# The last stage of a four-layer kernel: who adds the tokens, how its small steps are grouped, how its rows lie in memory, who issues its stores

## The chip, the cores and the metric

The kernel runs on one core of a Trainium2 chip. A core has TensorE (matmuls, PE in the profile), VectorE (DVE), ScalarE (ACT), GpSimd (POOL) and SyncE (SP), which here only issues transfers, and 16 DMA engines. The engines run their own instruction streams and meet at semaphores. The metric is the time of one execution on the device in microseconds, the median of several runs; lower is better.

## The reference

The input is 16 batches of 512 tokens, each of 128 float32 values. Four sublayers follow one another, each closed by a residual and a layer norm: a selective state-space layer, a layer with the signs of a 128x128 weight, gated linear attention with 16 heads, and a mixture of eight experts, of which each token takes two. The change touches only what comes after the experts have computed:

```python
out = jnp.sum(combined.reshape(-1, TOPK, D), axis=1)   # the token's two weighted results
...
x = _layernorm(x + _L1_ffn_ref(x, ...), axis=-1)
# _layernorm: (x - mean) / sqrt(var + 1e-5), over the 128 values of a token
```

So for every token: first result + second result + the token itself, then mean and variance over 128 values, then scale and shift.

## The kernel before

A long loop over batches computes the first three sublayers and sends each token, with its shares, to two rows of a scratch tensor that is sorted by expert. The expert stage then takes 136 tiles of 128 such rows, computes the expert of each tile, scales the rows by their shares, and writes them to `results_scratch` with indirect stores from GpSimd (L1997): first the results of every token's one expert, behind them those of the other. Beside it SP loads all tokens of the third sublayer back into `tokens` (L679).

The last stage, the tail, starts when all of these stores have landed. It goes over the 16 batches. A batch is 128 partitions x 4 tokens x 128 values. Token number c*128 + p of a batch lies on partition p (`"b (c p) d -> b p c d"`, L407, L538, L539), so each partition reads and writes four separate rows of 512 bytes. For batch b, with slot n = b modulo 4:

- SP loads the two result blocks into `both[:, n]` (`load_both`, L692), four batches at the start; the load of batch b + 4 is issued after VectorE has read batch b (`s_mixed`). Between these loads SP issues the store of batch b (L696), after its normalization (`s_final`).
- GpSimd adds the tokens to the second result in place (`add_token`, L2012), two batches ahead.
- VectorE adds the two results into `final_in[:, n]` (`mix_results`, L1819) and takes the statistics of each of the four tokens with `bn_stats` (L1829). Seven small steps on 128x4 (L1832 to L1841, `final_deviation`) make from them minus the mean and the variance of all four.
- GpSimd raises the variance to the power -1/2 (L2022) and multiplies it by minus the mean (L2024) (`final_shift`).
- ScalarE computes `final = final_in * scale + shift`, one activation a token column, four a batch (`normalize_final`, L1346), after the store that last used the slot has landed.

`final_in`, `final` and the small tensors have four slots (`FINAL_SLOTS`), and so has `both`. VectorE's result add of batch b waits for the normalization of batch b - 4. The order of the work is written out by hand: each engine runs its own loop over batches, in the order in which the instructions stand, and `LN_STEPS = 11` counts the semaphore's steps per batch (4 statistics, 7 small steps).

Of the kernel before, what the change touches and what calls it, by code (L numbers as in the profile page):

```python
# [7 lines left out]
P = 128  # L8
T = 512
TILES = T // P  # L10
# [24 lines left out]
LN_STEPS = 11  # L35
RMS_EPS = float(np.finfo(np.float32).eps)
# [171 lines left out]
FINAL_SLOTS = 4  # L208

# [18 lines left out]
def build(nc, a, out):  # L228
# [6 lines left out]
    with ExitStack() as ctx:  # L235
# [32 lines left out]
        minus_half = sb_kept("minus_half", [P, TILES])  # L268
# [11 lines left out]
        def sem(name):  # L280
# [114 lines left out]
        both = sb_kept("both", [P, FINAL_SLOTS, 2, TILES, P])  # L395
# [11 lines left out]
        x3_dram = nc.dram_tensor("x3_scratch", [B, T, P], F32, kind="Internal").ap().rearrange(  # L407
            "b (c p) d -> b p c d", p=P)
# [104 lines left out]
        s_both = [sem(f"both_results_loaded{n}") for n in range(FINAL_SLOTS)]  # L513
# [24 lines left out]
        out_dram = out.rearrange("b (c p) d -> b p c d", p=P)  # L538
        both_dram = results_dram[0:2 * B * T, :].rearrange("(r b c p) d -> r b p c d", r=2, b=B, p=P)  # L539
# [36 lines left out]
        def _(sp):  # L576
# [102 lines left out]
            def load_tokens(b):  # L679
                sp.dma_start(tokens[:, bass.ds(b * TILES, TILES), :],  # L680
                             x3_dram[bass.ds(b, 1)].rearrange("b p c d -> (b p) c d")).then_inc(s_tokens, 16)
# [10 lines left out]
            def load_both(b):  # L692
                for r in range(2):
                    sp.dma_start(both[:, b % FINAL_SLOTS, r, :, :], both_dram[r, b]).then_inc(s_both[b % FINAL_SLOTS], 16)

            def store(b, n):  # L696
                sp.wait_ge(s_final, TILES * (b + 1))
                sp.dma_start(out_dram[bass.ds(b, 1)].rearrange("b p c d -> (b p) c d"), final[:, n]
                             ).then_inc(s_out[n], 16)
# [3 lines left out]
            for b in range(FINAL_SLOTS):  # L703
                load_both(b)
            for b in range(B):
                store(b, b % FINAL_SLOTS)
                if b + FINAL_SLOTS < B:
                    sp.wait_ge(s_mixed, b + 1)
                    load_both(b + FINAL_SLOTS)
# [340 lines left out]
        def _(act):  # L1050
# [295 lines left out]
            def normalize_final(b):  # L1346
                n = b % FINAL_SLOTS
                act.wait_ge(s_shifted, b + 1)
                after(act, s_out[n], 16 * (b // FINAL_SLOTS))
                for t in range(TILES):  # L1350
                    nc.scalar.activation(final[:, n, t, :], final_in[:, n, t, :], ACT.Identity, bias=shift4[:, n, t:t + 1],
                                         scale=rstd4[:, n, t:t + 1]).then_inc(s_final, 1)

            for b in range(B):
                normalize_final(b)


        @block.vector
        def _(dve):
# [459 lines left out]
            def mix_results(b):  # L1819
                slot = b % FINAL_SLOTS  # L1820
                after(dve, s_final, TILES * (b - FINAL_SLOTS + 1))
                dve.wait_ge(s_added, b + 1)
                nc.vector.tensor_tensor(final_in[:, slot], both[:, slot, 0], both[:, slot, 1], ALU.add).then_inc(s_mixed, 1)

            def final_deviation(b):
                n = b % FINAL_SLOTS
                dve.wait_ge(s_mixed, b + 1)
                for t in range(TILES):
                    nc.vector.bn_stats(stats4[:, n, t, :], final_in[:, n, t, :]).then_inc(s_ln4, 1)  # L1829
                after(dve, s_shifted, b - FINAL_SLOTS + 1)  # L1830
                dve.wait_ge(s_ln4, at(b, LN_STEPS, 4))
# [3 lines left out]
                dve.wait_ge(s_ln4, at(b, LN_STEPS, 6))  # L1835
                nc.vector.tensor_tensor(apart4[:, n], apart4[:, n], apart4[:, n], ALU.mult).then_inc(s_ln4, 1)
                nc.vector.tensor_scalar(mean4[:, n], mean4[:, n], -0.5, None, ALU.mult).then_inc(s_ln4, 1)
                dve.wait_ge(s_ln4, at(b, LN_STEPS, 8))
                nc.vector.scalar_tensor_tensor(var4[:, n], apart4[:, n], P / 4, var4[:, n], ALU.mult, ALU.add).then_inc(s_ln4, 1)
                dve.wait_ge(s_ln4, at(b, LN_STEPS, 10))  # L1840
                nc.vector.tensor_scalar(var4[:, n], var4[:, n], 1 / P, LN_EPS, ALU.mult, ALU.add).then_inc(s_ln4, 1)  # L1841

            for b in range(B):
                mix_results(b)
                final_deviation(b)
# [3 lines left out]
        def _(pool):  # L1849
            nc.gpsimd.memset(minus_half[:], -0.5).then_inc(s_prep, 1)  # L1850
# [16 lines left out]
            def scale_of(step, scale, it):  # L1867

                pool.wait_ge(step, at(it, LN_STEPS, LN_STEPS))
                nc.gpsimd.tensor_tensor(rstd[:], var[:], minus_half[:], ALU.pow).then_inc(scale, 1)  # L1870
# [141 lines left out]
            def add_token(b):  # L2012
                slot = b % FINAL_SLOTS
                pool.wait_ge(s_both[slot], 32 * (b // FINAL_SLOTS + 1))
                nc.gpsimd.tensor_tensor(both[:, slot, 1, :, :], both[:, slot, 1, :, :], tokens[:, b * TILES:(b + 1) * TILES, :],
                                        ALU.add).then_inc(s_added, 1)

            def final_shift(b):
                n = b % FINAL_SLOTS
                pool.wait_ge(s_ln4, at(b, LN_STEPS, LN_STEPS))  # L2020
                after(pool, s_final, TILES * (b - FINAL_SLOTS + 1))
                nc.gpsimd.tensor_tensor(rstd4[:, n], var4[:, n], minus_half[:], ALU.pow).then_inc(s_rstd4, 1)  # L2022
                pool.wait_ge(s_rstd4, b + 1)
# [7 lines left out]
            pool.wait_ge(s_tokens, 16 * B)  # L2031
            for b in range(2):
                add_token(b)
            for b in range(B):
                final_shift(b)
                if b + 2 < B:
                    add_token(b + 2)
# [63 lines left out]
```

## Time and profile before

| | us |
|---|---|
| median of 3 runs | 2409.65 (2407.55 to 2413.64) |
| the profiled execution | 2408.81 |
| its span, first to last instruction | 2406.9 |
| busy: PE, DVE, ACT, POOL | 2090.9, 1953.4, 1414.8, 804.8 |
| the tail's first load issued, from the span's start | 2341.09 |

The page cuts the span in 40 slices of 60 us; a digit is the busy share in tenths. TensorE stands at 8 to 9 in the expert stage and at 0 in the last slice, where VectorE has 8, GpSimd 7 and ScalarE 4. The tail is thus the last slice and a little more. A time without a unit is in microseconds from the span's start. In the rows, `x4` counts instructions that are merged into one row, `[... <-X]` is the idle time of the engine before the row and what ended it, and L numbers are lines of the kernel before.

### The profile page before, as it was taken

Reading aid. Unit: us, or ns where it says so; the run is one execution under the profiler, and the core shown is the slowest. Engines: PE = TensorE matmul, PEld = TensorE weight load, DVE = VectorE, ACT = ScalarE, POOL = GpSimd, SP = SyncE. Lnnn points to the kernel's source line nnn. Section 1 sums busy time; section 2 is a strip of 40 time slices with the busy share of each in tenths; the row PEclk is TensorE's granted clock in tenths of the full one; section 3 lists DMA queues with packets and bytes.
Section 4 is the critical chain, followed back from the end, with each engine's and each line's share of the span. In section 5 each row is a group of like instructions: output and inputs, shape, how many; then the busy total and the mean of one; then the engine's idle time right before and its main releaser. Section 6 shows DMA issues by size and latency. Waiting matters only on the chain.

```text
span 2406.9 us, 52418 instructions
## 1 busy us (share of the span) xinstructions
PE 2090.9 (87%) x15864; PEld 1548.4 (64%) x15865; DVE 1953.4 (81%) x3681; ACT 1414.8 (59%) x3240; POOL 804.8 (33%) x1060
## 2 busy tenths in 40 slices
PE   4589899898989898989898999989889669999980
PEld 2256666575656575757565666657576569999980
DVE  6788988888898889898889898888985467777768
ACT  3466666666766666666676666667656323333334
POOL 0011414142424243232414141414243233333337
PEclk7699999999999999999999999999999879999995
DMA  6342424334242434242415242433321132212226
GB/s 178 88 115 63 111 75 101 90 81 104 68 105 66 116 74 114 68 109 71 116 55 127 56 115 73 103 88 84 102 67 30 61 119 61 59 54 62 60 58 188
DMA packets 154382, 212.88 MB, mean 88 GB/s; under 512 B 20296, under 2 KB 88912, under 8 KB 153920
## 3 DMA queue, kind: packets, MB, share of 16 engines
q1 hardware_dynamic: 132048, 144.20, 20.3%
q0 software_dynamic: 22272, 67.92, 13.8%
q8 instruction: 31, 0.51, 0.1%
q14 instruction: 31, 0.25, 0.0%
HBM read 134.71 MB, written 28.08 MB: 68 GB/s over the span
## 4 chain that ended last, share of the span: by engine, by line
PE 58%; DVE 18%; issue 9%; ACT 9%; DMA 4%; POOL 2%; DVEq 1%; SPq 0%; ACTq 0%; POOLq 0%
PE banks L1011 8%; PE banks L747 5%; PE banks L856 4%; PE banks L851 4%; PE banks L1022 4%; PE banks L835 4%; PE banks L886 4%; PE banks L908 4%; PE banks L881 3%; PE banks L804 3%; DVE ch L1449 2%; DVE push L1434 2%; ACT S L1190 2%; DMA y<-ch 2%; DVE hs L1441 2%
## 5 line engine op out<-in xcount | busy, mean ns | idle before, releaser
L1441 DVE TENSOR_TENSOR_SCAN hs<-decay,push 128x512 f32<-128x512 f32 x256 | 312.5, 1243 | 5.4
L1190 ACT ACTIVATE S<-banks,fall_tok 128x128 f32<-128x128 f32 x1024 | 277.7, 384 | 28.2 <-PE banks L823 26.4
L1011 PE MATMUL banks<-rowsT,w_here 128*128 128x128 f32 x2176 | 269.5, 278 | 6.6 <-DVE w_here L1785 6.1
L1011 PEld LDWEIGHTS banks<-rowsT,w_here 128*128 128x128 f32 x2176 | 256.0, 193 | 10.2 <-issue 9.4
L1956 POOL TENSOR_TENSOR qd<-q,q_fall 128x512 f32<-128x512 f32 x96 | 161.6, 1683 | 237.2 <-ACT chunk_fall L1175 237.1
L1865 POOL DMA_DIRECT2D y<-ch x96 | 88.1, 918 | 450.6 <-DVE ch L1449 349.4
L1547 DVE TENSOR_TENSOR S<-banks,S 128x512 f32<-128x512 f32 x256 | 168.0, 683 | 71.3 <-PE banks L835 43.1
L1997 POOL DMA_INDIRECT results_scratch<-rows_out,result_to x136 | 131.9, 970 | 241.3 <-ACT rows_out L1316 234.3
L1305 ACT ACTIVATE tanh_h<-banks 128x512 f32<-128x512 f32 x136 | 81.3, 598 | 203.5 <-PE banks L1011 162.4
L1434 DVE TENSOR_TENSOR push<-du,b_all 128x1024 f32<-128x1024 f32 x128 | 186.5, 1457 | 5.0 <-DMA b_all<-bc_scratch 4.4
L835 PE MATMUL banks<-q,k 64*128 64x128 f32 x1024 | 147.6, 284 | 43.9 <-DVE state L1598 28.9
L1101 ACT ACTIVATE decay<-delta,a_neg 128x512 f32<-128x512 f32 x256 | 171.9, 729 | 19.8 <-DVE hs L1441 19.4
L1934 POOL DMA_INDIRECT rows_scratch<-x,row_now x128 | 167.9, 1312 | 40.0 <-issue 34.2
L804 PE MATMUL banks<-x2T,w_k 128*128 128x512 f32 x256 | 134.6, 607 | 45.6 <-DVE k L1540 45.6
L1449 DVE TENSOR_TENSOR ch<-hs,c_all 128x1024 f32<-128x1024 f32 x128 | 163.4, 1276 | 3.0 <-DMA y<-ch 0.9
L1554 DVE SCALAR_TENSOR_TENSOR oT<-tog,banks 128x512 f32<-128x512 f32 x128 | 87.4, 683 | 93.6 <-ACT sq L1158 93.6
L835 PEld LDWEIGHTS banks<-q,k 64*128 64x128 f32 x1024 | 123.5, 187 | 58.8 <-issue 48.2
L851 PE MATMUL banks<-w_v,x2T 128*128 128x512 f32 x256 | 148.9, 665 | 0.0
L836 PE MATMUL banks<-q,k 64*128 64x128 f32 x1024 | 148.2, 285 | 0.0
L1870 POOL TENSOR_TENSOR rstd<-var,minus_half 128x4 f32<-128x4 f32 x48 | 48.7, 1014 | 296.6 <-DVE var L1415 296.6
L908 PEld LDWEIGHTS banks<-w_o,oT 128*128 128x128 f32 x1024 | 124.0, 193 | 36.4 <-issue 34.3
L1158 ACT ACTIVATE sq<-banks 128x512 f32<-128x512 f32 x128 | 76.9, 601 | 116.4 <-PE banks L886 116.4
(218 smaller groups left out, 5177.5 us busy)
## 6 DMA issues: line engine op xcount, KB each, us to landing
y<-ch POOLq DMA_DIRECT2D x96, 512.0 KB
b_all<-bc_scratch SPq DMA_DIRECT2D x128, 256.0 KB, 4.9
c_all<-bc_scratch SPq DMA_DIRECT2D x128, 256.0 KB
q_fall<-fall_scratch SPq DMA_DIRECT2D x192, 128.0 KB, 3.2
rows_in<-rows_scratch SPq DMA_DIRECT2D x136, 66.0 KB
both<-results_scratch SPq DMA_DIRECT2D x32, 256.0 KB, 3.4
w<-w_dram SPq DMA_DIRECT2D x3, 2048.0 KB, 9.1
xT<-xT_dram SPq DMA_DIRECT2D x16, 256.0 KB, 3.1
```

What stands on the lines that cost most here:

```text
L804: pe.matmul(bank, w[:, u * P:(u + 1) * P], x2T[:], start=True, stop=True).then_inc(full, 1)
L835: even = pe.matmul(low[:, at_h], k[0:DH, pair, here], q[0:DH, pair, here], start=True, stop=True)
L851: pe.matmul(bank, x2T[:, here], w_v[:, f * T:(f + 1) * T], start=True, stop=True).then_inc(full, 1)
L908: pe.matmul(bank[:, 0:P], oT[:, t, :], w_o[:, t, :], start=(t == 0), stop=(t == PAIRS - 1))
L1011: mm = pe.matmul(bank_h[:, u % 2, n, here], w_here[:, u % 2, n, here], x, start=True, stop=True)
L1101: nc.scalar.activation(decay[:, n % 2, h, :], delta[:, h, :], ACT.Exp, scale=a_neg[:, h, n:n + 1]).then_inc(s_decay, 1)
L1190: ins = nc.scalar.activation(S[:, g, here], bank[:, here], ACT.Exp, bias=fall_tok[:, head:head + 1])
L1434: nc.vector.tensor_tensor(push[:], du[:], b_all[:, slot, :].unsqueeze(1).broadcast_to([P, HALVES, T]), ALU.mult).then_inc(s_push, 1)
L1441: nc.vector.tensor_tensor_scan(hs[:, h, :], decay[:, n % 2, h, :], push[:, h, :], 0.0, ALU.mult, ALU.add).then_inc(s_scan, 1)
L1449: nc.vector.tensor_tensor(ch[:, n % 2, :, :], hs[:], c_all[:, slot, :].unsqueeze(1).broadcast_to([P, HALVES, T]), ALU.mult).then_inc(s_ch, 1)
L1547: nc.vector.tensor_tensor(S[:, g, :], full(ring, f"S{g}_{c}", j), S[:, g, :], ALU.mult).then_inc(ring.free_sem(f"S{g}_{c}"), 1)
L1934: nc.gpsimd.indirect_dma_start(out=rows_dram, out_offset=bass.IndirectOffsetOnAxis(ap=row_now[:, n, t:t + 1], axis=0), in_=x3_rows[:, t, : ...
```

## The change

- `BOTH_SLOTS = 8`: `both` has eight slots; the others keep four. SP issues the loads of batch b after VectorE has read batch b - 8, and no stores.
- Four tokens in a row per partition: token 4p + c of a batch lies on partition p in the tail (`"b (p c) d -> b p c d"`), so each partition reads and writes one piece of 2048 bytes, in the loads of results and tokens and in the store. The scratch tensor of tokens is still written in the old order of partitions, and read in the new one.
- VectorE adds the tokens (`add_token` is now VectorE's). It works in pairs of batches: two result adds, two token adds, eight statistics, and then the seven small steps once, on 128x8 (`PAIR_STEPS = 15`).
- GpSimd has only the pow and the product left, once per pair, on 128x8.
- ScalarE issues the store of batch b - 1 after the activations of batch b.

```diff
 LN_STEPS = 11
+PAIR_STEPS = 15
 RMS_EPS = float(np.finfo(np.float32).eps)
...
 FINAL_SLOTS = 4
+BOTH_SLOTS = 8
 
...
         eye = sb_kept("eye", [P, P])
-        minus_half = sb_kept("minus_half", [P, TILES])
+        minus_halves = sb_kept("minus_halves", [P, 2, TILES])
+        minus_half = minus_halves[:, 0]
         rms_eps = sb_kept("rms_eps", [P, 1])
...
         rows_out = sb_kept("rows_out", [P, 2, MOE_LOAD, P])
-        both = sb_kept("both", [P, FINAL_SLOTS, 2, TILES, P])
+        both = sb_kept("both", [P, BOTH_SLOTS, 2, TILES, P])
         stats4 = sb_kept("stats4", [P, FINAL_SLOTS, TILES, 6])
...
         fall_dram = nc.dram_tensor("fall_scratch", [B, 2, TILES, PAIRS, P], F32, kind="Internal").ap()
-        x3_dram = nc.dram_tensor("x3_scratch", [B, T, P], F32, kind="Internal").ap().rearrange(
-            "b (c p) d -> b p c d", p=P)
+        x3_scratch = nc.dram_tensor("x3_scratch", [B, T, P], F32, kind="Internal").ap()
+        x3_dram = x3_scratch.rearrange("b (c p) d -> b p c d", p=P)
+        tokens_dram = x3_scratch.rearrange("b (p c) d -> b p c d", p=P)
         rows_dram = nc.dram_tensor("rows_scratch", [ALL_ROWS, ROW], F32, kind="Internal").ap()
...
         s_results = [sem("results_stored0"), sem("results_stored1")]
-        s_both = [sem(f"both_results_loaded{n}") for n in range(FINAL_SLOTS)]
+        s_both = [sem(f"both_results_loaded{n}") for n in range(BOTH_SLOTS)]
         s_mixed = sem("results_mixed")
...
         x_dram = a["x"].rearrange("b (c p) d -> b p c d", p=P)
-        out_dram = out.rearrange("b (c p) d -> b p c d", p=P)
-        both_dram = results_dram[0:2 * B * T, :].rearrange("(r b c p) d -> r b p c d", r=2, b=B, p=P)
+        out_dram = out.rearrange("b (p c) d -> b p c d", p=P)
+        both_dram = results_dram[0:2 * B * T, :].rearrange("(r b p c) d -> r b p c d", r=2, b=B, p=P)
         spare_dram = rows_dram[EXPERTS * REGION:ALL_ROWS, :]
...
                 sp.dma_start(tokens[:, bass.ds(b * TILES, TILES), :],
-                             x3_dram[bass.ds(b, 1)].rearrange("b p c d -> (b p) c d")).then_inc(s_tokens, 16)
+                             tokens_dram[bass.ds(b, 1)].rearrange("b p c d -> (b p) c d")).then_inc(s_tokens, 16)
 
...
             def load_both(b):
+                slot = b % BOTH_SLOTS
                 for r in range(2):
-                    sp.dma_start(both[:, b % FINAL_SLOTS, r, :, :], both_dram[r, b]).then_inc(s_both[b % FINAL_SLOTS], 16)
-
-            def store(b, n):
-                sp.wait_ge(s_final, TILES * (b + 1))
-                sp.dma_start(out_dram[bass.ds(b, 1)].rearrange("b p c d -> (b p) c d"), final[:, n]
-                             ).then_inc(s_out[n], 16)
+                    sp.dma_start(both[:, slot, r, :, :], both_dram[r, b]).then_inc(s_both[slot], 16)
 
             for n in range(2):
                 sp.wait_ge(s_results[n], 16 * MOE_LOAD * (ROW_TILES // MOE_BODY))
-            for b in range(FINAL_SLOTS):
+            for b in range(B):
+                after(sp, s_mixed, b - BOTH_SLOTS + 1)
                 load_both(b)
-            for b in range(B):
-                store(b, b % FINAL_SLOTS)
-                if b + FINAL_SLOTS < B:
-                    sp.wait_ge(s_mixed, b + 1)
-                    load_both(b + FINAL_SLOTS)
             for n in range(FINAL_SLOTS):
...
                 n = b % FINAL_SLOTS
-                act.wait_ge(s_shifted, b + 1)
+                act.wait_ge(s_shifted, b // 2 + 1)
                 after(act, s_out[n], 16 * (b // FINAL_SLOTS))
                 for t in range(TILES):
                     nc.scalar.activation(final[:, n, t, :], final_in[:, n, t, :], ACT.Identity, bias=shift4[:, n, t:t + 1],
                                          scale=rstd4[:, n, t:t + 1]).then_inc(s_final, 1)
 
+            def store(b):
+                n = b % FINAL_SLOTS
+                act.wait_ge(s_final, TILES * (b + 1))
+                act.dma_start(out_dram[b], final[:, n]).then_inc(s_out[n], 16)
+
             for b in range(B):
                 normalize_final(b)
+                if b:
+                    store(b - 1)
+            store(B - 1)
 
...
                 after(dve, s_final, TILES * (b - FINAL_SLOTS + 1))
+                dve.wait_ge(s_both[b % BOTH_SLOTS], 32 * (b // BOTH_SLOTS + 1))
+                nc.vector.tensor_tensor(final_in[:, slot], both[:, b % BOTH_SLOTS, 0], both[:, b % BOTH_SLOTS, 1], ALU.add
+                                        ).then_inc(s_mixed, 1)
+
+            def add_token(b):
+                slot = b % FINAL_SLOTS
+                dve.wait_ge(s_mixed, b + 1)
+                nc.vector.tensor_tensor(final_in[:, slot], final_in[:, slot], tokens[:, b * TILES:(b + 1) * TILES, :], ALU.add
+                                        ).then_inc(s_added, 1)
+
+            def final_stats(b):
+                slot = b % FINAL_SLOTS
                 dve.wait_ge(s_added, b + 1)
-                nc.vector.tensor_tensor(final_in[:, slot], both[:, slot, 0], both[:, slot, 1], ALU.add).then_inc(s_mixed, 1)
-
-            def final_deviation(b):
-                n = b % FINAL_SLOTS
-                dve.wait_ge(s_mixed, b + 1)
                 for t in range(TILES):
-                    nc.vector.bn_stats(stats4[:, n, t, :], final_in[:, n, t, :]).then_inc(s_ln4, 1)
-                after(dve, s_shifted, b - FINAL_SLOTS + 1)
-                dve.wait_ge(s_ln4, at(b, LN_STEPS, 4))
+                    nc.vector.bn_stats(stats4[:, slot, t, :], final_in[:, slot, t, :]).then_inc(s_ln4, 1)
+
+            def final_deviation(m):
+
+                n = slice(2 * m % FINAL_SLOTS, 2 * m % FINAL_SLOTS + 2)
+                after(dve, s_shifted, m - 1)
+                dve.wait_ge(s_ln4, at(m, PAIR_STEPS, 8))
                 nc.vector.tensor_tensor(mean4[:, n], stats4[:, n, :, 1], stats4[:, n, :, 4], ALU.add).then_inc(s_ln4, 1)
                 nc.vector.tensor_tensor(apart4[:, n], stats4[:, n, :, 1], stats4[:, n, :, 4], ALU.subtract).then_inc(s_ln4, 1)
                 nc.vector.tensor_tensor(var4[:, n], stats4[:, n, :, 2], stats4[:, n, :, 5], ALU.add).then_inc(s_ln4, 1)
-                dve.wait_ge(s_ln4, at(b, LN_STEPS, 6))
+                dve.wait_ge(s_ln4, at(m, PAIR_STEPS, 10))
                 nc.vector.tensor_tensor(apart4[:, n], apart4[:, n], apart4[:, n], ALU.mult).then_inc(s_ln4, 1)
                 nc.vector.tensor_scalar(mean4[:, n], mean4[:, n], -0.5, None, ALU.mult).then_inc(s_ln4, 1)
-                dve.wait_ge(s_ln4, at(b, LN_STEPS, 8))
+                dve.wait_ge(s_ln4, at(m, PAIR_STEPS, 12))
                 nc.vector.scalar_tensor_tensor(var4[:, n], apart4[:, n], P / 4, var4[:, n], ALU.mult, ALU.add).then_inc(s_ln4, 1)
-                dve.wait_ge(s_ln4, at(b, LN_STEPS, 10))
+                dve.wait_ge(s_ln4, at(m, PAIR_STEPS, 14))
                 nc.vector.tensor_scalar(var4[:, n], var4[:, n], 1 / P, LN_EPS, ALU.mult, ALU.add).then_inc(s_ln4, 1)
 
-            for b in range(B):
-                mix_results(b)
-                final_deviation(b)
+            dve.wait_ge(s_tokens, 16 * B)
+            for m in range(B // 2):
+                for step in (mix_results, add_token, final_stats):
+                    for b in (2 * m, 2 * m + 1):
+                        step(b)
+                final_deviation(m)
 
 
         @block.gpsimd
         def _(pool):
-            nc.gpsimd.memset(minus_half[:], -0.5).then_inc(s_prep, 1)
+            nc.gpsimd.memset(minus_halves[:], -0.5).then_inc(s_prep, 1)
             nc.gpsimd.memset(one[:], 1.0).then_inc(s_prep, 1)
...
                 pool.wait_ge(step, at(it, LN_STEPS, LN_STEPS))
-                nc.gpsimd.tensor_tensor(rstd[:], var[:], minus_half[:], ALU.pow).then_inc(scale, 1)
+                nc.gpsimd.tensor_tensor(rstd[:], var[:], minus_half, ALU.pow).then_inc(scale, 1)
 
...
 
-            def add_token(b):
-                slot = b % FINAL_SLOTS
-                pool.wait_ge(s_both[slot], 32 * (b // FINAL_SLOTS + 1))
-                nc.gpsimd.tensor_tensor(both[:, slot, 1, :, :], both[:, slot, 1, :, :], tokens[:, b * TILES:(b + 1) * TILES, :],
-                                        ALU.add).then_inc(s_added, 1)
-
-            def final_shift(b):
-                n = b % FINAL_SLOTS
-                pool.wait_ge(s_ln4, at(b, LN_STEPS, LN_STEPS))
-                after(pool, s_final, TILES * (b - FINAL_SLOTS + 1))
-                nc.gpsimd.tensor_tensor(rstd4[:, n], var4[:, n], minus_half[:], ALU.pow).then_inc(s_rstd4, 1)
-                pool.wait_ge(s_rstd4, b + 1)
+            def final_shift(m):
+                n = slice(2 * m % FINAL_SLOTS, 2 * m % FINAL_SLOTS + 2)
+                pool.wait_ge(s_ln4, at(m, PAIR_STEPS, PAIR_STEPS))
+                after(pool, s_final, 2 * TILES * (m - 1))
+                nc.gpsimd.tensor_tensor(rstd4[:, n], var4[:, n], minus_halves[:], ALU.pow).then_inc(s_rstd4, 1)
+                pool.wait_ge(s_rstd4, m + 1)
                 nc.gpsimd.tensor_tensor(shift4[:, n], mean4[:, n], rstd4[:, n], ALU.mult).then_inc(s_shifted, 1)
...
                     shares_of(t // MOE_LOAD + 1)
-            pool.wait_ge(s_tokens, 16 * B)
-            for b in range(2):
-                add_token(b)
-            for b in range(B):
-                final_shift(b)
-                if b + 2 < B:
-                    add_token(b + 2)
+            for m in range(B // 2):
+                final_shift(m)
 
```

## Rows read from the trace of the kernel before

**Rows 1.** The chain of waits, 2300 us to the end: start us, us, what.

```profile
2334.69 0.91 PE banks L1022 x8
...
2338.78 2.24 DMA results_scratch<-rows_out,result_to
...
2341.52 3.33 DMA both<-results_scratch
```

**Rows 2.** The timeline, start of the tail: start us, us, engine, instruction [idle before].

```profile
2341.09 5.80 SPq L694 DMA_DIRECT2D both<-results_scratch  x8
...
2344.99 1.25 POOL L2015 TENSOR_TENSOR both<-both,tokens 128x512 f32<-128x512 f32 x1 [5.25 <-DMA both<-results_scratch]
...
2346.28 0.69 DVE L1823 TENSOR_TENSOR final_in<-both 128x512 f32<-128x512 f32 x1 [9.52 <-POOL both L2015]
...
2347.85 1.26 POOL L2015 TENSOR_TENSOR both<-both,tokens 128x512 f32<-128x512 f32 x1 [1.60 <-DMA both<-results_scratch]
```

**Rows 3.** The timeline, one batch in the middle of the tail.

```profile
2377.33 0.69 DVE L1823 TENSOR_TENSOR final_in<-both 128x512 f32<-128x512 f32 x1
2377.40 0.38 SPq L698 DMA_DIRECT2D out_dram<-final  x1
2377.50 1.40 POOL L2022 TENSOR_TENSOR rstd<-var,minus_half 128x4 f32<-128x4 f32 x1 [0.58 <-DVE var L1841]
2378.05 0.87 DVE L1829 BATCH_NORM_STATS2 stats<-final_in 128x6 f32<-128x128 f32 x4
...
2379.03 0.17 DVE L1832 TENSOR_TENSOR mean<-stats 128x4 f32<-128x4 f32 x1
2379.12 1.28 POOL L2015 TENSOR_TENSOR both<-both,tokens 128x512 f32<-128x512 f32 x1
2379.19 1.24 DVE L1834 TENSOR_TENSOR var<-stats 128x4 f32<-128x4 f32 x1
2379.20 1.65 ACT L1351 ACTIVATE final<-final_in,shift,rstd 128x128 f32<-128x128 f32 x4 [1.83 <-POOL shift L2024]
...
2380.81 0.69 DVE L1823 TENSOR_TENSOR final_in<-both 128x512 f32<-128x512 f32 x1
```

**Rows 4.** The timeline, the last two batches.

```profile
2398.37 1.01 POOL L2022 TENSOR_TENSOR rstd<-var,minus_half 128x4 f32<-128x4 f32 x1 [0.57 <-DVE var L1841]
...
2398.57 0.69 DVE L1823 TENSOR_TENSOR final_in<-both 128x512 f32<-128x512 f32 x1 [0.28 <-ACT final L1351]
...
2400.27 0.17 DVE L1832 TENSOR_TENSOR mean<-stats 128x4 f32<-128x4 f32 x1
...
2400.43 0.16 DVE L1834 TENSOR_TENSOR var<-stats 128x4 f32<-128x4 f32 x1
...
2400.94 0.17 DVE L1841 TENSOR_SCALAR var<-var 128x4 f32<-128x4 f32 x1
...
2402.51 1.65 ACT L1351 ACTIVATE final<-final_in,shift,rstd 128x128 f32<-128x128 f32 x4 [1.17 <-POOL shift L2024]
```

**Rows 5.** Busy time by window: PE, PEld, DVE, ACT, POOL, PEclk, DMA share, GB/s.

```profile
2343.00:2345.00 2.00, 0.00 (x0) 0.00 (x0) 0.00 (x0) 0.00 (x0) 0.01 (x1) 0.50 1.06 308
2363.00:2383.00 20.00, 0.00 (x0) 0.00 (x0) 18.96 (x73) 9.01 (x23) 16.07 (x19) 0.50 0.80 226
```

**Rows 6.** The timeline, attention stage: adds in a row, and both engines at once.

```profile
1098.05 1.29 DVE L1491 TENSOR_TENSOR y<-y,sz 128x512 f32<-128x512 f32 x2
...
1185.76 1.49 DVE L1449 TENSOR_TENSOR ch<-hs,c_all 128x1024 f32<-128x1024 f32 x1
...
1186.10 2.27 POOL L1956 TENSOR_TENSOR qd<-q,q_fall 128x512 f32<-128x512 f32 x1
...
1187.17 2.28 DVE L1434 TENSOR_TENSOR push<-du,b_all 128x1024 f32<-128x1024 f32 x1
```

**Rows 7.** The timeline, a pow over one column.

```profile
1115.17 0.56 POOL L1879 TENSOR_TENSOR rms<-rms,minus_half 128x1 f32<-128x1 f32 x1
```

**Rows 8.** DMA of the first 25 us, in 40 slices.

```profile
GB/s 0 0 26 189 96 275 321 220 23 109 115 229 154 29 91 151 354 400 406 307 81 112 249 334 374 419 419 419 419 413 319 199 199 196 235 402 484 123 270 87
```

## The prediction

> **What bounds the kernel now.** I read the 40 slices first: TensorE is idle in the last slice, so the change touches only a tail in which nothing else is computed. The chain of waits from 2300 us on then names the stages: matmuls until 2335 us, 2.24 us for the last scatter to land at 2341.02, and from there mostly VectorE rows [rows 1]. The tail is 2341.09 to the end of the span, 2406.9: 65.8 us. It has three pieces.
>
> The start is a transfer: loads issued from 2341.09, GpSimd's first add at 2344.99, VectorE's first at 2346.28, and the second batch ready only at 2347.85 [rows 2].
>
> The middle is a loop of 3.48 us per batch (2377.33 to 2380.81), VectorE busy in nearly all of it [rows 3]. In it are 0.72 us of result add, 0.98 us from the first statistic to the first small step, and small steps that take 0.75 us in the last batch (2400.27 to 2400.94, plus 0.08 to the next start) but 1.78 us in every batch before [rows 3, 4]. The difference, 1.03 us, is one 128x4 add that lasts 1.24 us instead of 0.16. It starts 0.07 us after GpSimd's add over 128x512 and ends with it. In the last batch GpSimd has no add, and the step lasts 0.16 us [rows 4]. So the two engines exclude each other for operations with two inputs in on-chip memory. GpSimd pays too: its pow lasts 1.39 us beside VectorE's add and 1.01 us alone [rows 3, 4]. What sets the end here is VectorE, with 1.03 us of each round spent waiting for GpSimd's add.
>
> ScalarE works 1.65 us of each round and DMA is at a share of 0.80 and 226 GB/s [rows 3, 5]; both have room.
>
> The end: last small step 2400.94, pow and shift, four activations from 2402.51 to 2404.16, then 2.74 us of store and final wait [rows 4].
>
> **The change, part by part.**
>
> *Token add on VectorE, small steps once per two batches.* Adds with two inputs run 0.60 us apart (two in 1.29 us, each 0.69) [rows 6]. Per pair: 4 adds, 2.40 us; 8 statistics, 0.98 for the first four and about 0.82 for four more (0.87 less the overlap), 1.80; small steps 0.75, taken as unchanged at 128x8 because a step of 0.16 us is not made of its four elements. Sum 4.95 us per pair, 2.48 per batch against 3.48. GpSimd's add and VectorE's 1.03 us of waiting go.
>
> *What GpSimd still costs.* In the attention stage both engines want the shared access in turn: VectorE's add over 1024 runs from 1185.76, GpSimd's product is issued at 1186.10 and VectorE's next at 1187.17; GpSimd goes first and ends at 1188.37, and VectorE's ends 1.08 us after it, 2.28 us in all [rows 6]. So a waiting GpSimd instruction is served between two VectorE ones even when these are back to back. With four adds in a row, the pow is served after the first one. How long does it hold VectorE? The one place that shows it: the pow at 2398.37, VectorE's last result add at 2398.57, which lasts 0.69 us, not stretched, while the pow runs to 2399.38 [rows 4]. The pow lets go after at most some 0.2 us. The shift (0.20 us) is a plain product and can hold its whole length. Both ends for GpSimd's hold per pair: 0 and 0.4 us if the pow behaves so; I take 0.15, since both overlap VectorE's own 0.09 us drain. The other reading of the pow is a rival below.
>
> The Trainium skill, "SBUF — State Buffer", section "Who interferes with whom", says that a VectorE instruction with two SBUF inputs and a GpSimd instruction that reads SBUF exclude each other, and that the first holds the pair for the whole instruction. By this rule, the trace agrees for the adds (1.24 against 0.16 us) and disagrees for the pow (0.69 us at 0.20 us into it). With the rule the sum per pair would be 4.95 + 1.6 + 0.2 = 6.75 us, not 5.1.
>
> *Pow over eight columns.* 0.56 us for 128x1 and 1.01 for 128x4 [rows 4, 7]: 0.15 us a column, so 1.61 us for 128x8. Ends: 1.01 (nothing per column) and 2.02 (twice 1.01). I take 1.61.
>
> *The buffer loop: what is late next.* final_in keeps four slots, which are now two pairs, and the second result add of pair m+2 waits for the second normalization of pair m. Call T the start of the first result add after pair m's small steps. Pow issued T+0.17, served at T+0.6, done T+2.2; shift issued 2.3, waits for the token add then running, done 2.7; ScalarE starts 2.75, first batch 1.65 us, one store issue, second batch 1.65 us. The store issue on ScalarE is shown nowhere; on SP it takes 0.38 us, and eight load issues take 5.80 us, 0.77 apart [rows 2, 3]. Bounds 0 (hidden under the last activation) and 0.77; I take 0.3, nearest to the 0.38 row, which is a store of the same bytes. So the pair is normalized at T + L with L = 6.35 us (5.4 to 7.3 by the ends). From that second result add to the next T VectorE needs 4.95 - 0.60 = 4.35 us, 4.50 with the hold. A round of VectorE alone is 5.10; the loop through ScalarE spans two pairs, (L + 4.50)/2 = 5.42 us. The loop is the longer: **5.4 us per pair, 2.7 per batch**. The stall stands at VectorE's second result add of a pair, some 0.3 us per pair, released by ScalarE. The ends give 4.95 and (7.3 + 4.75)/2 = 6.0.
>
> The other added waits. A normalization waits for the store four batches back; a store is issued one batch late, after the next normalization, but for the odd batches there are still some 5 us to the reuse, and a store lands in about 2.7 us (2404.17 to the end). Behind that wait stand ScalarE's next batch and stores, so stores that land later than 5 us would be felt in L. GpSimd's wait for the pair two back and VectorE's for its shift are met some 4 us early.
>
> *2 KB rows, eight slots.* Before, the window 2343 to 2345 moved 308 GB/s at full share with 512 B rows; 4 KB weight rows moved up to 419 [rows 5, 8]. 786 KB per batch in 2.7 us is 291 GB/s: below both, and eight slots (4.2 MB, 14 us at 300 GB/s) let the loads run well ahead. I put it at nothing in the middle. If rows of 2 KB gained nothing, 308 still suffices. At the start it counts: four loads issued 0.77 apart end at 2343.8 and land by about 2346.2 instead of 2347.85. The token loads and the one memset lie beside matmuls: nothing. SP loses its stores, which nobody waited for.
>
> *Sum.* First result add 2344.7; second 2346.2; T of pair 1 at 2346.2 + 4.35 = 2350.55; seven pairs more, 7 x 5.42 = 37.9: 2388.5. Tail: 0.17 + 1.61 + 0.08 + 0.20 + 0.04, then 1.65 + 0.3 + 1.65, then 2.7: 8.4 us (5.8 + 0.6 for the pow and 2.0 for a second batch in the last group). Span 2396.9, 10.0 us less than 2406.9. The profiled execution took 2408.81 us, so 2398.8; the median of the runs is 0.84 above that: **2399.6 us**.
>
> **Rivals.**
>
> A. *The loop is not felt* (pow near 1.0 us, store issue hidden): 5.0 us per pair, tail 7.5, end 2350.55 + 35 + 7.5 = 2393.1, time 2395.8. For it: each term has its lower end in a row. Against: the 128x1 row says that pow grows with its columns.
>
> B. *ScalarE is late*: store issue 0.77, pow 2.0, L 7.3: 6.0 us per pair, tail 9.3, end 2401.9, time 2404.6. For it: the 0.77 row. Against: the stores have 0.38.
>
> C. *The pow holds VectorE to its end*, as GpSimd's add does: 4.95 + 1.61 + 0.20 = 6.76 per pair, end 2350.55 + 47.3 + 8.4 = 2406.3, time 2409: no change. For it: the 1.24 us rows; this is what the skill's rule gives. Against: the single 0.69 us row.
>
> D. *Slower*: C with a pow of 2.02 us. Place: VectorE's second result add in each pair, behind the pow; price 2.2 us a pair; 7.17 per pair, end 2350.55 + 50.2 + 8.8 = 2409.6, time 2412.3. It decides from a hold of 1.8 us per pair, where 7 pairs use up what the tail leaves (6.8 us each).
>
> E. *DMA paces it*: if reads of results beside stores stay at the 226 GB/s of the middle [rows 5], the 11.5 MB due before the last batch need 51 us from 2341.5; with 4.35 and the tail of 8.4 the end is near 2406, time 2408. Against: that rate was at share 0.80, demand-limited; windows at full share show 308.
>
> **Chances.** Forecast (5.1 to 5.7 us a pair) 0.60, A 0.13, B 0.13, C 0.06, D 0.04, E 0.04. A bound of 0.3%, 7.2 us, is about what a measurement of this kernel can tell from no change. The forecast's own range is 2397 to 2402; nearly all of it, A, and a third of B lie below 2402.4: faster 0.74; same 0.22 (rest of B, C, E, the edge of the forecast); slower 0.04. The range takes in A and most of B: 2394.5 to 2404.5.
>
> **What would show it.** In the tail: no GpSimd add; small VectorE steps all near 0.16 us; pow once per pair at 1.6 us plus up to 0.5 of waiting; pairs 5.4 us apart; one result add per pair released by ScalarE's normalization; loads far ahead. Rows that prove me wrong: a result add stretched by over 1 us beside the pow (C, D), VectorE idle behind loads (E), or ScalarE's groups over 0.6 us apart within a pair (B).

## The result, and the profile after

The changed kernel took 2399.59 us in the median of five runs (2393.74 to 2402.78), the kernel before 2413.06 on the same occasion (2407.55 to 2413.64). The ratio is 0.9948 with a 95% interval from 0.9933 to 0.9964: faster by about half a per cent, 12.5 us by the ratio and 13.5 us by the medians. Forecast were 2399.6 us and 10.0 us less. That the time agrees to 0.01 us is luck: the forecast started from a median before of 2409.65 us, which is 3.4 us below the one of five runs, and the gain is larger by as much.

The profiled execution of the changed kernel took 2393.74 us, its span 2391.9. Runs of one kernel differ by up to 9 us, and the profiles show where: the work before the tail, the same in every kernel here but for the order in which tokens are loaded, ends anywhere between 2336.7 and 2349.7 us. The tail of the changed kernel was 53.6 and 54.3 us in two profiles, so the tail is the measure from here on: from the first load of results issued to the end of the span. It was 65.8 us before and is now 2391.9 - 2338.27 = 53.6 us, 12.2 less. Line numbers in the rows of this part are those of the kernel that the row is from.

The timeline at the start of the tail, changed kernel (it answers [rows 2]):

```profile
2338.27 22.21 SPq L699 DMA_DIRECT2D both<-results_scratch  x32
2341.84 0.69 DVE L1827 TENSOR_TENSOR final_in<-both 128x512 f32<-128x512 f32 x1 [7.88 <-DMA both<-results_scratch]
2343.64 0.69 DVE L1827 TENSOR_TENSOR final_in<-both 128x512 f32<-128x512 f32 x1 [1.10 <-DMA both<-results_scratch]
...
2347.89 1.29 DVE L1827 TENSOR_TENSOR final_in<-both 128x512 f32<-128x512 f32 x2
2348.07 2.04 POOL L2034 TENSOR_TENSOR rstd<-var,minus_halves 128x8 f32<-128x8 f32 x1 [11.13 <-DVE var L1856]
...
2352.74 0.69 DVE L1827 TENSOR_TENSOR final_in<-both 128x512 f32<-128x512 f32 x1
```

VectorE's second add runs 5.37 us after the first issue (5.1 forecast). The rows at 2347.89 and 2348.07 decide rival C: two result adds in a row take 1.29 us, as they do alone [rows 6], while a pow runs beside them. GpSimd waits for the first add (2.04 us instead of 1.64) and does not stretch the second.

One pair in the middle (it answers [rows 3]):

```profile
2363.24 0.69 DVE L1827 TENSOR_TENSOR final_in<-both 128x512 f32<-128x512 f32 x1
2363.41 2.02 POOL L2034 TENSOR_TENSOR rstd<-var,minus_halves 128x8 f32<-128x8 f32 x1 [2.54 <-DVE var L1856]
2364.12 0.69 DVE L1827 TENSOR_TENSOR final_in<-both 128x512 f32<-128x512 f32 x1 [0.19 <-ACT final L1347]
2364.73 1.28 DVE L1833 TENSOR_TENSOR final_in<-final_in,tokens 128x512 f32<-128x512 f32 x2
2365.50 0.57 POOL L2036 TENSOR_TENSOR shift<-mean,rstd 128x8 f32<-128x8 f32 x1
2365.93 1.64 DVE L1840 BATCH_NORM_STATS2 stats<-final_in 128x6 f32<-128x128 f32 x8
2366.11 0.49 ACT L1347 ACTIVATE final<-final_in,shift,rstd 128x128 f32<-128x128 f32 x1 [2.02 <-POOL shift L2036]
2366.12 0.34 ACTq L1353 DMA_DIRECT2D out_dram<-final  x1
2366.51 1.63 ACT L1347 ACTIVATE final<-final_in,shift,rstd 128x128 f32<-128x128 f32 x4
2367.67 0.17 DVE L1847 TENSOR_TENSOR mean<-stats 128x8 f32<-128x8 f32 x1
...
2367.78 0.34 ACTq L1353 DMA_DIRECT2D out_dram<-final  x1
...
2368.05 1.25 ACT L1347 ACTIVATE final<-final_in,shift,rstd 128x128 f32<-128x128 f32 x3
...
2368.44 0.69 DVE L1827 TENSOR_TENSOR final_in<-both 128x512 f32<-128x512 f32 x1
...
2369.33 0.69 DVE L1827 TENSOR_TENSOR final_in<-both 128x512 f32<-128x512 f32 x1 [0.19 <-ACT final L1347]
```

A pair takes 5.20 us (2363.24 to 2368.44), 2.6 per batch against 3.48. No small step is long. The loop of the forecast is there: T = 2363.24, the pow is done at T + 2.19, ScalarE starts at T + 2.87 and ends at 2369.30, and VectorE's second add of the next pair but one follows at 2369.33, T + 6.09. From there to the next T are 4.32 us (2369.33 to 2373.65), and (6.09 + 4.32)/2 = 5.21.

Its waits from 2352 us on (engine, line, what it waited for: us, times, longest):

```profile
POOL rstd L2034 <- DVE var L1856: 17.7, 7, 2.5
ACT final L1347 <- POOL shift L2036: 13.4, 7, 2.0
DVE final_in L1827 <- ACT final L1347: 1.2, 6, 0.3
```

Only the last row is on the path: six pairs, all released by ScalarE. Two result adds of a pair start 0.88 us apart (2363.24, 2364.12) instead of 0.60, so a pair loses 0.28 us; 0.3 were forecast.

Windows of the changed kernel, columns as in [rows 5]:

```profile
2345.00:2353.00 8.00, 0.00 (x0) 0.00 (x0) 7.86 (x36) 2.52 (x7) 2.39 (x3) 0.50 1.05 387
2353.00:2363.00 10.00, 0.00 (x0) 0.00 (x0) 9.29 (x37) 5.95 (x16) 5.18 (x4) 0.50 1.05 395
2363.00:2383.00 20.00, 0.00 (x0) 0.00 (x0) 18.78 (x72) 11.91 (x31) 10.37 (x8) 0.50 0.35 133
```

With rows of 2 KB the full share carries 387 to 395 GB/s (the first window has only loads in it, but for one store at its end); in the third window the loads are done and only stores are left.

The end (it answers [rows 4]):

```profile
2383.99 0.17 DVE L1856 TENSOR_SCALAR var<-var 128x8 f32<-128x8 f32 x1
2384.24 1.64 POOL L2034 TENSOR_TENSOR rstd<-var,minus_halves 128x8 f32<-128x8 f32 x1 [2.54 <-DVE var L1856]
...
2388.13 1.25 ACT L1347 ACTIVATE final<-final_in,shift,rstd 128x128 f32<-128x128 f32 x3
2389.41 0.34 ACTq L1353 DMA_DIRECT2D out_dram<-final  x1
```

From 2384.07 (last step plus 0.08) to the end are 7.8 us, 8.4 forecast.

### The profile page after: what moved, and what is told of

The parts are those of the page before. It is cut to its first block, busy times and chain, and to the rows that moved or that the text cites. A ratio compares the mean times of both kernels' runs of the same rounds, so it can differ in the third digit from the quotient of the medians.

```text
span 2391.9 us, 52206 instructions
## 1 busy us (share of the span) xinstructions
PE 2080.7 (87%) x15736; PEld 1547.6 (65%) x15865; DVE 1942.9 (81%) x3641; ACT 1415.4 (59%) x3240; POOL 784.3 (33%) x1028
## 4 chain that ended last, share of the span: by engine, by line
PE 54%; DVE 17%; issue 9%; ACT 8%; DMA 2%; POOL 2%; DVEq 1%; SPq 0%; ACTq 0%; POOLq 0%
PE banks L1007 8%; PE banks L852 4%; PE banks L1018 4%; PE banks L847 4%; PE banks L904 4%; PE banks L743 4%; PE banks L882 4%; PE banks L831 4%; PE banks L877 3%; DVE ch L1453 3%; DVE push L1438 2%; PE banks L800 2%; DVE hs L1445 2%; PE banks L819 2%; ACT S L1186 2%
## 5 line engine op out<-in xcount | busy, mean ns | idle before, releaser
L1438 DVE TENSOR_TENSOR push<-du,b_all 128x1024 f32<-128x1024 f32 x128 | 192.0, 1500 | 6.0 <-DMA b_all<-bc_scratch 5.9
L1888 POOL TENSOR_TENSOR rstd<-var,minus_halves 128x4 f32<-128x4 f32 x48 | 48.7, 1015 | 296.4 <-DVE var L1419 296.4
```

Of the source, the lines that this page charges most:

```text
L1438: nc.vector.tensor_tensor(push[:], du[:], b_all[:, slot, :].unsqueeze(1).broadcast_to([P, HALVES, T]), ALU.mult).then_inc(s_push, 1)
```

## The experiments

All were profiled, once each; "pair" is the mean time of two batches in the middle, "second add" the time from the first load issued to VectorE's second result add, "rest" the time from there to the end.

| kernel | tail us | second add | rest | pair |
|---|---|---|---|---|
| before | 65.8 | | | 6.96 |
| changed | 53.6 | 5.4 | 48.3 | 5.21 |
| changed, again | 54.3 | 6.1 | 48.2 | 5.21 |
| before, VectorE adds tokens | 60.3 | | | 6.36 |
| changed, GpSimd adds tokens | 54.4 | 7.3 | 47.2 | 5.31 |
| changed, small steps per batch | 58.1 | 5.8 | 52.3 | 5.87 |
| changed, 512-byte rows | 54.6 | 6.0 | 48.5 | 5.21 |
| changed, four slots of results | 54.2 | 6.0 | 48.3 | 5.21 |
| changed, SP's stores | 54.2 | 6.0 | 48.2 | 5.21 |
| changed, six slots of final_in | 53.5 | 6.6 | 46.9 | 4.93 |
| six slots, first and last pair | 50.7 | 6.2 | 44.5 | 4.93 |
| the same, one add on GpSimd | 48.0 | 6.3 | 41.8 | 4.45 |

The second add varies by 1.3 us (5.37 to 6.63) between kernels whose first loads are the same; the rest varies by 0.1 between the four whose pairs take 5.21 us and whose rows have 2 KB. So kernels are compared by the rest where it means the same work. In the last two rows and in "GpSimd adds tokens" it does not: there other work stands before the second add.

**VectorE adds the tokens, nothing else changed.**

```diff
 def mix_results(b):
-    dve.wait_ge(s_added, b + 1)
+    dve.wait_ge(s_both[slot], 32 * (b // FINAL_SLOTS + 1))
     nc.vector.tensor_tensor(final_in[:, slot], both[:, slot, 0], both[:, slot, 1], ALU.add).then_inc(s_mixed, 1)
+    dve.wait_ge(s_mixed, b + 1)
+    nc.vector.tensor_tensor(final_in[:, slot], final_in[:, slot], tokens[...], ALU.add).then_inc(s_added, 1)
...
-                if b + 2 < B:                           # GpSimd
-                    add_token(b + 2)
...
```

> The kernel before with one part of the change: VectorE adds the tokens, GpSimd keeps only pow and product. Batch by batch, four slots, 512-byte rows, stores by SP. Tail is counted from the first load of results issued to the end of the span; it is 65.8 us before and 53.6 us with the whole change. Theory (VectorE's long small step is GpSimd's add excluding it): all small steps near 0.16 us, a round of 0.72 + 0.72 + 0.98 + 0.75 = 3.17 us instead of 3.48, tail 3.9 + 16 x 3.17 + 5.9 = 60.5 us. Rival (the long step has another cause): it stays, the add comes on top, 4.2 us a round, tail 77 us.

The tail was 60.3 us. In the timeline of this kernel a round in the middle is 3.18 us and the step that lasted 1.24 us lasts 0.16:

```profile
2373.35 0.69 DVE L1823 TENSOR_TENSOR final_in<-both 128x512 f32<-128x512 f32 x1
...
2374.08 0.69 DVE L1825 TENSOR_TENSOR final_in<-final_in,tokens 128x512 f32<-128x512 f32 x1
...
2375.94 0.16 DVE L1837 TENSOR_TENSOR var<-stats 128x4 f32<-128x4 f32 x1
...
2376.53 0.69 DVE L1823 TENSOR_TENSOR final_in<-both 128x512 f32<-128x512 f32 x1
```

VectorE does more and is done sooner: GpSimd's add had been the cause. Of the 5.5 us, 1.4 are gained at the start, where VectorE's first add no longer follows one of GpSimd (3.77 us after the first load issued instead of 5.19).

**The adds back on GpSimd in the changed kernel.** The other way round, `add_token` on GpSimd, two pairs ahead:

```diff
-for step in (mix_results, add_token, final_stats):      # VectorE
+for step in (mix_results, final_stats):
 for m in range(B // 2):                                 # GpSimd
     final_shift(m)
+    for b in (2 * m + 4, 2 * m + 5):
+        if b < B:
+            add_token(b)
...
```

> The changed kernel with the token adds put back on GpSimd, two pairs ahead; pairs, eight slots, 2 KB rows and ScalarE's stores stay. Theory (exclusion): VectorE needs 1.2 + 1.8 + 0.75 = 3.75 us a pair, but its small steps meet GpSimd's two adds and two of them are stretched by 1 us or more: 5.8 to 6.0 us a pair against 5.21, tail near 60 us. Rival (exclusion costs little when the adds are spread): GpSimd's own 2 x 1.28 + 2.0 + 0.25 sets 4.9 to 5.0 us a pair, tail near 53 us.

A miss: 54.4 us, 5.31 a pair, nearer to the rival. The timeline of one pair:

```profile
2367.86 2.50 POOL L2039 TENSOR_TENSOR both<-both,tokens 128x512 f32<-128x512 f32 x2
...
2368.39 0.76 DVE L1841 TENSOR_TENSOR mean<-stats 128x8 f32<-128x8 f32 x1
2369.08 0.16 DVE L1842 TENSOR_TENSOR apart<-stats 128x8 f32<-128x8 f32 x1
2369.16 1.24 DVE L1843 TENSOR_TENSOR var<-stats 128x8 f32<-128x8 f32 x1
...
2371.15 1.29 DVE L1827 TENSOR_TENSOR final_in<-both 128x512 f32<-128x512 f32 x2 [0.27 <-ACT final L1347]
```

The exclusion is there, but nearly half of the first add falls beside the statistics, which have one input and don't notice (eight in 1.63 us). The stretch is 0.6 + 1.08 us, against 1.2 us for two adds on VectorE, and VectorE waits for ScalarE once in the whole tail (0.27 us, the last row). Once the batches go in pairs, who adds the tokens is worth 0.1 us a pair; alone it was worth 0.6. The tails say the same: 54.4 us against 53.6 and 54.3.

**Small steps, pow and product per batch.**

```diff
-                final_deviation(m)
+                final_deviation(2 * m)
+                final_deviation(2 * m + 1)
...
```

> The changed kernel with the small steps, pow and product per batch again (128x4), after the pair's adds and statistics. Theory: 0.75 us more of VectorE a pair, but the loop through ScalarE no longer closes, since the first batch's pow starts earlier: 4.85 + 0.75 = 5.6 us a pair against 5.21, no wait of result adds for ScalarE; the last group is one batch with a pow of 1.0 us, so the end is 2.1 us shorter. Tail 10.4 + 7 x 5.6 + 5.7 = 55.3 us against 53.6. Rival (the loop through ScalarE and the last group cost as much as the steps save): tail 53.6 or less.

58.1 us, 5.87 a pair, no wait for ScalarE: the theory's side, but 2.8 us more than its 55.3. The rows of its timeline:

```profile
2369.60 1.29 DVE L1827 TENSOR_TENSOR final_in<-both 128x512 f32<-128x512 f32 x2
...
2372.01 1.63 DVE L1840 BATCH_NORM_STATS2 stats<-final_in 128x6 f32<-128x128 f32 x8
...
2373.75 0.17 DVE L1847 TENSOR_TENSOR mean<-stats 128x4 f32<-128x4 f32 x1
...
2374.42 0.17 DVE L1856 TENSOR_SCALAR var<-var 128x4 f32<-128x4 f32 x1
...
2374.69 0.19 DVE L1847 TENSOR_TENSOR mean<-stats 128x4 f32<-128x4 f32 x1
...
2375.46 1.29 DVE L1827 TENSOR_TENSOR final_in<-both 128x512 f32<-128x512 f32 x2
```

The second group starts 0.27 us behind the last step of the first, since it waits for that step's count, where a result add follows after 0.08. So the small steps of a pair take 1.71 us in two groups (2373.75 to 2375.46) and 0.77 in one (2367.67 to 2368.44 above), 0.94 more and not 0.75. VectorE's own pair without the wait for ScalarE is 4.93 us, as the run with six slots shows further down, and 4.93 + 0.94 is the 5.87.

**The layout.**

```diff
-out_dram = out.rearrange("b (p c) d -> b p c d", p=P)
+out_dram = out.rearrange("b (c p) d -> b p c d", p=P)
```

and the same for `both_dram` and `tokens_dram`.

> The changed kernel with the old order of tokens: four rows of 512 bytes per partition in results, tokens and stores. Theory: rate falls from 395 to some 290 to 308 GB/s and loads are issued 0.77 us apart instead of 0.43, but eight slots and a need of 302 GB/s keep the middle at 5.21 us a pair; only the second batch comes later, by 1.4 us: tail 55.0 us. Rival (DMA becomes the pace): result adds wait for loads in the middle, 5.5 us a pair or more, tail 57 us or more.

54.6 us, pairs of 5.21; 55.0 us was expected, with a second batch 1.4 us later than it came in the changed kernel, and it came 0.7 us later (6.0 us). The window at full load shows the lower rate. The rest is 0.3 us longer (48.54 against 48.26), and that is the last store: from its issue to the end are 2.8 us (2391.64 to 2394.4), with 2 KB rows 2.5 (2389.41 to 2391.9).

```profile
2353.00:2363.00 10.00, 0.00 (x0) 0.00 (x0) 9.33 (x38) 6.08 (x16) 5.17 (x4) 0.50 1.20 310
2363.00:2383.00 20.00, 0.00 (x0) 0.00 (x0) 18.68 (x76) 12.74 (x32) 9.61 (x8) 0.50 0.82 237
```

**Four slots of results** (`BOTH_SLOTS = 4`) and **stores issued by SP**:

```diff
-            for b in range(B):
-                after(sp, s_mixed, b - BOTH_SLOTS + 1)
-                load_both(b)
+            for b in range(BOTH_SLOTS):
+                load_both(b)
+            for b in range(B):
+                store(b)
+                if b + BOTH_SLOTS < B:
+                    sp.wait_ge(s_mixed, b + 1)
+                    load_both(b + BOTH_SLOTS)
```

> The changed kernel with four slots of results instead of eight. Theory: a slot's loads are issued four batches, 10.4 us, ahead and land in 3 to 6 us, so nothing waits: tail 53.6 us, up to 0.3 either way, no result add released by DMA after the second. Rival (the eight slots carry the middle): result adds of later batches wait for loads, 1 us or more in all.

> The changed kernel with the stores issued by SP, each before the load eight batches on. Theory (ScalarE's issue is hidden: its activations stay 0.39 us apart beside the issue): tail 53.6 us, up to 0.3 either way, pairs 5.21 us apart. Rival (the issue lengthens the loop through ScalarE): without it each pair is 0.15 to 0.4 us shorter, tail 51 to 52.6 us.

Both 54.2 us, with rests of 48.3 and 48.2. The tails are 0.3 us above the range expected, since the second batch came at 6.0 us and not at 5.4; by the rest neither part is worth anything here. Without stores on ScalarE its eight activations of a pair take what they take with them, 3.19 us (2366.11 to 2369.30 above):

```profile
2375.65 3.19 ACT L1356 ACTIVATE final<-final_in,shift,rstd 128x128 f32<-128x128 f32 x8 [2.02 <-POOL shift L2037]
```

**Six slots of final_in.**

```diff
-        final_in = sb_kept("final_in", [P, FINAL_SLOTS, TILES, P])
+        final_in = sb_kept("final_in", [P, IN_SLOTS, TILES, P])      # 6
-                after(dve, s_final, TILES * (b - FINAL_SLOTS + 1))
+                after(dve, s_final, TILES * (b - IN_SLOTS + 1))
...
```

> The changed kernel with six slots of final_in instead of four, so that the second result add of a pair no longer waits for the pair two back. Theory (loop through ScalarE): pairs 4.85 us apart instead of 5.21, six of them, tail 51.4 us, no result add released by ScalarE. Rival (another wait is right behind, such as the stores or GpSimd's pow): tail 52.5 to 53.6 us with VectorE idle elsewhere.

The wait is gone, and the pair is 4.93 us. The tail as a whole, 53.5 us, missed its 51.4 and lies in the rival's range. Of the 2.1 us, 1.3 are the second batch, which came late this time (6.6 us), 0.5 are pairs of 4.93 and not 4.85, and 0.3 one pair of 5.26 in which VectorE paused between two small steps; no run shows why. The rest is shorter by 1.4 us. The rows:

```profile
2378.23 1.30 DVE L1828 TENSOR_TENSOR final_in<-both 128x512 f32<-128x512 f32 x2
2378.39 2.02 POOL L2035 TENSOR_TENSOR rstd<-var,minus_halves 128x8 f32<-128x8 f32 x1 [2.54 <-DVE var L1857]
2379.45 1.28 DVE L1834 TENSOR_TENSOR final_in<-final_in,tokens 128x512 f32<-128x512 f32 x2
```

Here the pow meets back-to-back adds in every round. The token adds start 1.22 us behind the result adds, twice the 0.60 of [rows 6] but for 0.02: this is all that the pow costs VectorE. The pair is still 4.93 and not the 4.85 of the changed kernel's second pair. The 0.08 lie between the first statistic and the first small step (1.74 against 1.66 us), where from the third pair on the code has one more wait, for `s_shifted`; the changed kernel has the same two times, before and from the third pair on. That this wait is the cause is argued, since no run leaves it out.

**A better version, in two steps.** First both ends of the loop, on top of the six slots of final_in, beside the changed kernel on the same chip:

```diff
+                if m == 0:
+                    for b in (0, 1):
+                        mix_results(b)
+                        add_token(b)
+                        final_stats(b)
...
+                        if m == B // 2 - 1:
+                            final_deviation(m, b)
...
```

> The changed kernel itself, for comparison on the same chip. Tail 53.6 to 54.9 us, as the second batch lands 5.4 to 6.6 us after the first load is issued in the profiles so far; from the second result add to the end 48.3 us. Faster than before by 10 to 13 us.

> The changed kernel with three edits of the loop's ends: six slots of final_in; in the first pair VectorE finishes batch 0's adds and statistics before it takes batch 1; in the last pair small steps, pow and product are per batch. By the profile: 1.4 us from the six slots, about 0.5 from the first pair (work put into the wait for batch 1), about 0.5 from the last (VectorE 1.1 us more, ScalarE's last group one batch and a pow of 1.0: 1.6 less). Tail 51.0 to 52.3 us, 2.4 us faster than the changed kernel. Rival (the ends don't matter, the loop does): 52.2 to 53.5 us.

Changed kernel 2398.68 us, ratio 0.9948 (0.9935 to 0.9961); this one 2392.07 us, ratio 0.9918 (0.9905 to 0.9930), tail 50.7 us, 0.3 below its range. Against the run with six slots alone, the first pair gave 1.1 us (3.12 instead of 4.25 us from the second result add to the second pair) and the last 1.3 us (11.55 instead of 12.81 us from its first result add to the end), where 0.5 us each were expected. Then one token add of each pair on GpSimd, put where it meets only one-input work:

```diff
                 nc.gpsimd.tensor_tensor(rstd4[:, n], var4[:, n], minus_halves[:], ALU.pow).then_inc(s_rstd4, 1)
+                b = 2 * m + 5
+                if b < B:
+                    slot = b % BOTH_SLOTS
+                    pool.wait_ge(s_both[slot], 32 * (b // BOTH_SLOTS + 1))
+                    nc.gpsimd.tensor_tensor(both[:, slot, 1], both[:, slot, 1], tokens[...], ALU.add).then_inc(s_early, 1)
                 pool.wait_ge(s_rstd4, m + 1)
```

> e7 with the token add of every odd batch from 5 on moved to GpSimd, between its pow and its product, so that it falls beside VectorE's statistics, which have one input. Theory (only VectorE's two-input operations and GpSimd's reads exclude each other): VectorE has 0.6 us less in six pairs, 4.3 us a pair, no small step over 0.3 us; tail 48 us, 6 us faster than the changed kernel. Rival (the add slips under the small steps, as with both adds on GpSimd): a step stretched by 0.5 to 1.2 us a pair, tail 51 to 54 us.

2389.73 us, ratio 0.9913 (0.9899 to 0.9928), tail 48.0 us. The timeline shows the add beside the statistics, both at full speed; it ends 0.26 us before the first small step, which lasts 0.17 us:

```profile
2364.46 1.30 DVE L1835 TENSOR_TENSOR final_in<-both 128x512 f32<-128x512 f32 x2
...
2366.40 1.64 DVE L1853 BATCH_NORM_STATS2 stats<-final_in 128x6 f32<-128x128 f32 x8
2366.63 1.25 POOL L2064 TENSOR_TENSOR both<-both,tokens 128x512 f32<-128x512 f32 x1
...
2368.14 0.17 DVE L1861 TENSOR_TENSOR mean<-stats 128x8 f32<-128x8 f32 x1
...
2368.92 1.30 DVE L1835 TENSOR_TENSOR final_in<-both 128x512 f32<-128x512 f32 x2
```

The pair is 4.45 us where 4.3 were expected: the adds before the statistics take 1.94 us (2364.46 to 2366.40) instead of 2.42, 0.48 less and not 0.6. The intervals of the last two versions overlap; by the tails the second is 2.7 us shorter.

## Why the prediction was right

- *VectorE waits 1.03 us of each round for GpSimd's add.* Shown, by taking only that add away from GpSimd: 5.5 us of the tail for a part that puts an add on the engine that sets the end. But this worth hangs on the order of the edits: with the batches in pairs, the adds could have stayed on GpSimd (54.4 us against 53.6 and 54.3). The prediction saw the wait rightly and did not ask what pairs alone would make of it.
- *Small steps once per pair.* Shown: going back costs 4.5 us (58.1 against 53.6, of which 0.4 is the start). Between the two lie 2.2 us (60.3 to 58.1) that come from the rest: adds and statistics in a row, 6.36 to 5.87 us a pair, less what the first pair loses by waiting for two batches. The rows show where the 0.49 us lie: a token add starts 0.73 us behind the result add of its own batch (2373.35 and 2374.08), and adds in a row start 0.60 us apart. The three make up the 12.2; this middle part was not tried alone.
- *VectorE alone, 4.95 us a pair.* The second pair, which waits for nobody, took 4.85 (2347.89 to 2352.74); from the third on it would be 4.93, by the run with six slots. The small steps over eight columns take 0.77 us, as forecast no more than over four.
- *The pow holds VectorE at most 0.2 us.* Right, and less: 0.15 us a pair taken, 0.02 seen, so rivals C and D fell.
- *The pow over eight columns, 1.61 us.* It takes 1.64.
- *The loop through ScalarE is the bound, L = 6.35.* Right, 6.09. The term that was off is the store issue: 0.3 us taken, nothing measured, since it lies under a running activation. Two batches take ScalarE 3.19 us, not 3.6; ScalarE starts 0.12 us later than forecast. With the smaller hold this makes 5.22 us instead of 5.42 in six rounds, 1.2 us; the round before them, which waits for nobody, took 4.85, 0.6 us less; the end is 0.6 us shorter, of which ScalarE's two batches are some 0.4. With a start 0.2 us later, this is the 2.2 us by which the tail is shorter than forecast. Of rival A one condition came true, the hidden issue, and the other, a pow near 1.0 us, did not.
- *Layout, eight slots and ScalarE's stores are worth nothing in the middle.* Right: the rest changes by 0.3, 0.0 and 0.0 us, and the 0.3 are the last store, not the middle. At the start the forecast let the second batch land 1.65 us sooner through the layout; the same kernel has since shown 5.4 and 6.1 us, with 512-byte rows 6.0, so no gain from it is shown. An issue of a load did become shorter, 0.43 us in the median against 0.83 with 512-byte rows in the same kernel. The 419 GB/s that the forecast took as the most for 4 KB rows is not the highest slice of [rows 8], which has 484; nothing in the sum hangs on it.

The Trainium skill, "SBUF — State Buffer", section "Who interferes with whom", says that issue order decides who blocks and that the first holds the shared pair for its whole instruction. Of GpSimd's adds this is so in the kernel before and in the changed one with the adds on GpSimd (1.24 us for a 0.16 us step). Of its pow it is not: adds issued into it run at 1.29 us for two. The measurement decides.

## What to carry to other kernels

Look for short operations that last as long as something on the other engine: a two-input VectorE step of 1.24 us was a GpSimd add of 1.28. Two cures worked: the add on VectorE, and, better, the add on GpSimd at a place where VectorE works with one input. Before pairing rounds, count the slots: the loop through the last reader, (latency + own work)/2 for two pairs, may close before the engine is full. And find out which of several edits carry the time, by taking each back from the whole and not only by adding it to the start: here layout, slots and stores carried nothing, the pairs carried most, and the engine of the token add was worth 5.5 us without the pairs and next to nothing with them.

## What the runs showed of the hardware that was not expected

- ScalarE's store issue of 0.34 us does not delay its activations: they stay 0.39 us apart, and the issue, which stands behind four activations in the program, starts beside the first of them (2366.12 and 2366.11).
- GpSimd's pow over 128x8 takes 1.64 us but lets VectorE's two-input adds through; a plain add of 1.25 us doesn't.
- Transfers at the full share ran at 387 to 395 GB/s in pieces of 2 KB, at 308 to 310 in pieces of 512 bytes.
